# A graph layer on one core: x and edges also handed in transposed, first stage for G alone

## The reference

```python
Q = relu(x @ Wq + bq);  V = x @ Wv + bv                 # x: 6250 x 512, float32
Q = relu(layer_norm(Q));  H = sum(Q, axis=1, keepdims=True) ** 2
H = pi / (2 * 2 * (max(H) - min(H))) * H
c, s = Q * cos(H), Q * sin(H)
out = c @ (c.T @ V) + s @ (s.T @ V)
norm = c @ sum(c, axis=0)[:, None] + s @ sum(s, axis=0)[:, None] + 1e-10
# edges: src, dst (106250, sorted by dst), and one loop of each node
deg = segment_sum(ones, dst);  coef = rsqrt(deg)[src] * rsqrt(deg)[dst]
gcn = segment_sum((x @ Wg)[src] * coef, dst) + bg
y = relu(layer_norm(out / norm + gcn + V) * gamma + beta)
return layernorm(x + y)
```

## Time and profile before

| | us |
|---|---|
| median of 3 runs (lowest to highest) | 1565.83 (1563.94 to 1568.54) |
| span of the profiled execution, first to last instruction | 1564.0 |
| TensorE matmuls busy, x7911 | 1493.1 (95%) |
| VectorE busy | 1060.7 (68%) |
| GpSimd busy | 921.2 (59%) |
| ScalarE busy | 497.6 (32%) |

### The profile page before, as it was taken

The page is one execution under the profiler, slowest core; times in us unless marked ns, Lnnn a source line. Parts: engine busy times, 40 slices in busy tenths (PEclk is TensorE's granted clock), DMA queues, the critical chain, the costliest instruction groups (busy, mean ns, idle before and its releaser), DMA issues.

```text
span 1564.0 us, 24480 instructions
## 1 busy us (share of the span) xinstructions
PE 1493.1 (95%) x7911; PEld 942.9 (60%) x7911; DVE 1060.7 (68%) x2945; ACT 497.6 (32%) x1010; POOL 921.2 (59%) x1022
## 2 busy tenths in 40 slices
PE   5999999899999997999998999989999999999995
PEld 3777788666666663444443444437777777767763
DVE  6999577677777676444445544457878877878785
ACT  2322776533333222111111111113333333333332
POOL 0000000277777775777776777777777777777772
PEclk9999999999999997999999999999999999999997
DMA  6555544699999998889888999889999999999894
GB/s 237 183 183 183 175 157 150 235 311 311 331 309 331 299 325 246 286 286 302 284 285 260 292 296 307 294 248 314 298 290 311 304 294 294 312 288 309 279 315 130
DMA packets 172753, 423.84 MB, mean 271 GB/s; under 512 B 24142, under 2 KB 25802, under 8 KB 172616
## 3 DMA queue, kind: packets, MB, share of 16 engines
q0 software_dynamic: 71120, 236.74, 48.1%
q1 hardware_dynamic: 79980, 146.16, 27.3%
q10 hardware_dynamic: 21516, 39.29, 6.6%
HBM read 351.42 MB, written 70.67 MB: 270 GB/s over the span
## 4 chain that ended last, share of the span: by engine, by line
PE 83%; DMA 6%; DVE 6%; issue 2%; ACT 2%; POOL 1%; SPq 0%; POOLq 0%; DVEq 0%; ACTq 0%
PE bank L1320 18%; PE bank L1321 17%; PE bank L1322 17%; PE bank L1436 12%; PE bank L1438 11%; DMA gathered<-scaled_g,index_slots 3%; DVE stage L948 2%; PE bank L1567 1%; PE bank L1376 1%; DMA stage<-in_x 1%; PE bank L1363 1%; POOL gathered L550 1%; DMA combine<-values 1%; PE bank L1504 1%; PE bank L1507 1%
## 5 line engine op out<-in xcount | busy, mean ns | idle before, releaser
L550 POOL DMA_INDIRECT gathered<-scaled_g,index_slots x882 | 882.9, 1001 | 305.7 <-issue 187.7
L1066 DVE TENSOR_SCALAR one_hot<-iota_bf,dst_in_tile,gathered 128x128 bf16<-128x128 bf16 x882 | 268.8, 326 | 327.4 <-DMA gathered<-scaled_g,index_slots 300.5
L1320 PE MATMUL bank<-weights,operands 128*128 128x512 f32 x784 | 395.5, 504 | 6.6 <-DVE stage L966 6.1
L1436 PE MATMUL bank<-gathered,one_hot 128*128 128x512 f16 x882 | 344.1, 390 | 25.7 <-DVE one_hot L1066 25.6
L1438 PE MATMUL bank<-gathered,one_hot 128*128 128x512 f16 x882 | 339.0, 384 | 0.0
L1321 PE MATMUL bank<-weights,operands 128*128 128x512 f32 x784 | 311.3, 397 | 0.0
L1322 PE MATMUL bank<-weights,operands 128*128 128x512 f32 x784 | 310.7, 396 | 0.0
L535 POOL COPY dst_slots<-dst_cols 128x18 f32 x49 | 13.9, 284 | 301.8 <-issue 299.6
L1320 PEld LDWEIGHTS bank<-weights,operands 128*128 128x128 f32 x784 | 149.1, 190 | 69.4 <-DVE stage L966 7.0
L1436 PEld LDWEIGHTS bank<-gathered,one_hot 128*128 128x128 bf16 x882 | 85.9, 97 | 171.1 <-issue 74.9
L707 ACT ACTIVATE operands_f<-operands,cos_sin_v 128x512 f16<-128x512 f32 x98 | 69.5, 720 | 335.8 <-PE bank L1322 201.6
(11 more groups left out here) (231 smaller groups left out, 1916.3 us busy)
## 6 DMA issues: line engine op xcount, KB each, us to landing
operands<-values SPq DMA_DIRECT2D x98, 256.0 KB, 5.7
stage<-in_x SPq DMA_DIRECT2D x96, 256.0 KB, 3.8
turned_x<-operands SPq DMA_DIRECT2D x37, 512.0 KB, 3.1
operands<-turned_x SPq DMA_DIRECT2D x37, 512.0 KB, 6.4
gathered<-scaled_g,index_slots POOLq DMA_INDIRECT x882, 5.2
scaled_g<-pairs SPq DMA_DIRECT2D x49, 260.0 KB, 2.1
pairs<-scaled_g SPq DMA_DIRECT2D x49, 260.0 KB
values<-stage ACTq DMA_DIRECT2D x49, 256.0 KB, 4.8
```

Source lines behind the costliest of these rows:

```text
L550: pool.indirect_dma_start(out=plain(row_ring[k % RING]), out_offset=None, in_=table, in_offset=bass.IndirectOffsetOnAxis(ap=index_slots[:, ...
L1066: dve.tensor_scalar(one_hot[:, k % HOT, :], iota_bf[:, :], column(dst_in_tile, seq % 2 * PER_TILE + k), scale_of(row), ALU.is_equal, ALU.m ...
L1320: pe.matmul(out_ap, a_hi, b_hi, start=start and n == 0, stop=False, skip_group_check=True)
L1436: pe.matmul(gcn_banks[seq % 2][:, :], one_hot[:, k % HOT, :], hi, start=k == 0, stop=False, skip_group_check=True)
```

## The change

- The host hands in, beside x, x in transposed tiles (`x_turned`), src and dst with a column for each chunk of 128 edges (`src_by_chunk`, `dst_by_chunk`), and dst padded (`dst_flat`). The transposes of x and of the edges on TensorE, their copies out of PSUM, and the DRAM copy of the transposed x go.
- First stage: SP loads the transposed tile to where the rest will be, four tiles in turn, when the tile four before is multiplied. ScalarE rounds it (`g_round`), GpSimd subtracts the rounded part from it in place (`g_split`), before which GpSimd waits for src and copies it. VectorE waits for GpSimd's tile t before the compares of tile t.
- All 49 tiles of Q and V are in the run, one every 16/3 steps. SP loads the transposed x again (256 KB), ScalarE rounds it (`x_round`), VectorE subtracts (`x_split`). The square of V moves from VectorE to ScalarE.
- The own row is added to V from G in SBUF when V is made (`own_sum`) and stored (`own_values`); `own_load` and `add_own` go, and the combine load takes that sum.
- The sweeps are spread over the steps anew: 20/7 steps a tile for cosine and sine, 27/4 for the output.

The core of the diff:

```diff
-    FUSED = 12
-    QV_TILES = TILES - FUSED
     QV_RING = 3
     STEPS = TILES * PER_TILE
-    HEAD, DRAIN = 6 * QV_RING, 24
-    LAST_QV = 6 * (QV_TILES - 1 - QV_RING)
+    HEAD, DRAIN = 18, 24
+
+    def qv_at(t):
+        return 16 * (t - QV_RING) // 3
+
+    LAST_QV = qv_at(TILES - 1)
...
-    COS_END = COS_AT + 10 * (TILES - 1) // 3 + 3
+
+    def cos_at(t):
+        return COS_AT + 20 * t // 7
+
+    COS_END = cos_at(TILES - 1) + 3
     SIN_AT = COS_END + 6
-    SIN_END = SIN_AT + 3 * (TILES - 1) + 3
+
+    def sin_at(t):
+        return SIN_AT + 20 * t // 7
+
+    SIN_END = sin_at(TILES - 1) + 3
     OUT_AT = SIN_END + 6
-    assert B == 4 and TAIL and FULL == 48 and SCALED < QV_TILES and OUT_AT + 7 * FULL < STEPS
+
+    def out_at(n):
+        return OUT_AT + 27 * n // 4
+
+    assert B == 4 and TAIL and FULL == 48 and out_at(FULL) + 7 < STEPS and qv_at(0) >= -HEAD
...
             def g_load(t):
-                r, n = rows_of(t), x_slot(t)
-                if t in (WIDE + 2, WIDE + 3):
-                    sp.wait_ge(s["degrees_summed"], 1)
-                else:
-                    sp.wait_ge(s["g_x_turned"], freed(t, 2 if t < WIDE + 2 else 4))
-                sp.dma_start(stage[0:r, n, :], dram_rows(x, t, r)).then_inc(g_x_loaded[n], 16)
+                sp.wait_ge(s["g_summed"], freed(t, XT_RING))
+                sp.dma_start(operands_raw[:, 4 + t % XT_RING, :], x_turned[t, :, :]).then_inc(g_x_loaded[t % XT_RING], 16)
 
             def raw_load(raw, weight, arrived):
                 sp.dma_start(raw, weight.rearrange("(k p) n -> p k n", p=P)).then_inc(s[arrived], 16)
 
-            g_load(0)
-            g_load(1)
-            full_groups(src, src_nat, s["src_loaded"])
-            last_group(src, src_nat, s["src_loaded"])
+            sp.dma_start(dst_i, dst_by_chunk).then_inc(s["dst_loaded"], 16)
+            for t in range(XT_RING):
+                g_load(t)
             raw_load(raws[1], Wq, "q_raw_loaded")
             raw_load(raws[2], Wv, "v_raw_loaded")
+            sp.dma_start(src_i, src_by_chunk).then_inc(s["src_loaded"], 16)
...
+            def x_load(t):
+                if t < XT_RING:
+                    sp.wait_ge(s["g_summed"], done(TILES - XT_RING + t))
+                else:
+                    sp.wait_ge(s["q_summed"], freed(t, XT_RING))
+                sp.dma_start(operands_raw[:, 4 + qv_slot(t), :], x_turned[t, :, :]).then_inc(x_loaded[t % XT_RING], 16)
...
             for t in range(0, TILES):
-                if t <= WIDE:
-                    g_load(t + 2)
-                if t == WIDE:
-                    g_load(t + 3)
-                if t >= WIDE and t + 4 < TILES:
-                    g_load(t + 4)
-                if t < QV_TILES:
-                    xt_store(t)
+                if t + XT_RING < TILES:
...
-                if seq == 0:
-                    sp.wait_ge(s["v_squared"], done(FUSED - 1))
+                sp.wait_ge(own_stored[seq % QV_RING], 16 * (seq // QV_RING + 1))
                 sp.wait_ge(s["combined_stored"], seq * 16)
-                sp.dma_start(combine[:, :], dram_rows(values, seq, P)).then_inc(s["combine_loaded"], 16)
+                sp.dma_start(combine[:, :], dram_rows(own_values, seq, P)).then_inc(s["combine_loaded"], 16)
...
+            pool.wait_ge(s["src_loaded"], 16)
+            pool.tensor_copy(src_cols[:, :], src_i).then_inc(s["src_kept"], 1)
+            pool.sem_inc(s["g_x_split"], LEAD)
+
+            def g_split(t):
+                rest, raw = operands[:, 4 + t % XT_RING, :], operands_raw[:, 4 + t % XT_RING, :]
+                pool.wait_ge(s["g_x_hi"], done(t))
+                pool.tensor_tensor(rest, raw, plain(operands[:, t % XT_RING, :]), ALU.subtract)\
+                    .then_inc(s["g_x_split"], 1)
+
+            for t in range(TILES):
+                g_split(t)
 
...
-            def g_step(t, n, r):
-                turned = banks[1 + n][:, :].rearrange("p (b c) -> p b c", c=P)[:, :, 0:r]
-                x_hi = operands[:, t % 4, :].rearrange("p (b c) -> p b c", c=P)[:, :, 0:r]
-
-                act.wait_ge(s["g_x_turned"], done(t))
-                act.wait_ge(s["g_summed"], freed(t, 4))
-                if t - 4 < QV_TILES:
-                    act.wait_ge(xt_stored[t % 4], t // 4 * 16)
-                else:
-                    act.wait_ge(s["q_summed"], done(nth(t - 4)))
-                act.copy(x_hi, turned).then_inc(s["g_x_hi"], 1)
-
-            def g_keep(t, n, r):
+            def g_round(t):
+                act.wait_ge(g_x_loaded[t % XT_RING], t // XT_RING * 16 + 16)
+                act.copy(operands[:, t % XT_RING, :], operands_raw[:, 4 + t % XT_RING, :]).then_inc(s["g_x_hi"], 1)
+
+            def x_round(t):
+                act.wait_ge(x_loaded[t % XT_RING], t // XT_RING * 16 + 16)
+                act.copy(operands[:, qv_slot(t), :], operands_raw[:, 4 + qv_slot(t), :]).then_inc(s["x_hi"], 1)
...
+            def own_store(t):
+                act.wait_ge(s["own_summed"], done(t))
+                act.dma_start(dram_rows(own_values, t, P), own_room(t)).then_inc(own_stored[t % QV_RING], 16)
+
+            def v_square(t):
+                act.wait_ge(s["v_kept"], done(t))
+                if t > 0:
+                    act.wait_ge(s["v_squared"], done(t - 1))
+                act.activation(squares_out, v_room(t), ACT.Square, accum_out=column(row_v_square, t))\
+                    .then_inc(s["v_squared"], 1)
 
...
-                for t, at in in_flight(qv_at, QV_TILES, q):
+                for t, at in in_flight(qv_at, TILES, q):
+                    if at == 1 and t + 1 < TILES:
+                        x_round(t + 1)
+                    if at == late(t, 5):
+                        v_store(t)
+                        v_square(t)
                     if at == 6:
-                        v_store(t)
+                        own_store(t)
...
-            def g_split(t, n, r):
-                turned = banks[1 + n][:, :].rearrange("p (b c) -> p b c", c=P)[:, :, 0:r]
-                x_hi = operands[:, t % 4, :].rearrange("p (b c) -> p b c", c=P)[:, :, 0:r]
-                x_lo = operands[:, 4 + t % 4, :].rearrange("p (b c) -> p b c", c=P)[:, :, 0:r]
-                dve.wait_ge(s["g_x_hi"], done(t))
-                dve.tensor_tensor(x_lo, turned, plain(x_hi), ALU.subtract).then_inc(s["g_x_split"], 1)
+            def x_split(t):
+                rest, raw = operands[:, 4 + qv_slot(t), :], operands_raw[:, 4 + qv_slot(t), :]
+                dve.wait_ge(s["x_hi"], done(t))
+                dve.tensor_tensor(rest, raw, plain(operands[:, qv_slot(t), :]), ALU.subtract)\
+                    .then_inc(s["x_split"], 1)
...
+            def own_sum(t):
+                if t == 0:
+                    for n in range(PAIRS):
+                        dve.wait_ge(pair_stored[n], 16 * len(range(n, TILES, PAIRS)))
+                dve.wait_ge(own_stored[t % QV_RING], t // QV_RING * 16)
+                dve.wait_ge(s["v_kept"], done(t))
+                dve.scalar_tensor_tensor(own_room(t), q_tile(t), column(own_scale, t), v_room(t), ALU.mult, ALU.add)\
+                    .then_inc(s["own_summed"], 1)
...
-            g_split(0, 0, P)
-            g_split(1, 1, P)
             for t in range(0, TILES):
+                dve.wait_ge(s["g_x_split"], done(t))
                 if t < HIST_TILES:
-                    bins(3 * t)
-                keep_beside_g(t)
-                if t + 2 < TILES:
-                    g_split(t + 2, t % 2, rows_of(t + 2))
-                if t < HIST_TILES:
-                    bins(3 * t + 1)
-                    bins(3 * t + 2)
-                beside_g(t)
+                    for third in range(3):
+                        bins(3 * t + third)
                 between_tiles(t)
             for n in range(pairs_until(TILES - 2), pairs_until(TILES - 1)):
                 pair_split(n)
             for group in FACTOR_GROUPS:
                 if group[2] == TILES:
...
-            def add_own(seq):
-
-                dve.wait_ge(s["combine_loaded"], seq * 16 + 16)
-                dve.wait_ge(s["own_loaded"], seq * 16 + 16)
-                link = linked("own_linked", seq, 1)
-                hi, lo = halves(own_rows)
-                link(dve.scalar_tensor_tensor(combine[:, :], hi, column(own_scale, seq), combine[:, :],
-                                              ALU.mult, ALU.add))
-                dve.scalar_tensor_tensor(combine[:, :], lo, column(own_scale, seq), combine[:, :],
-                                         ALU.mult, ALU.add).then_inc(s["own_added"], 1)
-
...
-            def qv_beside_g(t):
-                if t == QV_TILES:
-                    pe.wait_ge(s["raw_split"], 1 + 2 * B)
-                else:
-                    pe.wait_ge(s["v_kept"], done(nth(t) - 1))
-                x_product(banks[5], t % 4, range(B), 2).then_inc(s["v_summed"], 1)
-                if t > QV_TILES:
-                    pe.wait_ge(s["q_biased"], done(nth(t) - 1))
```

(15 more changed lines are left out.)

366 lines of the change are left out of this document (123 added, 243 removed).

## The result

| | us |
|---|---|
| median after (4 runs, 1579.27 to 1582.29) | 1580.19 |
| median before, beside it (4 runs, 1563.94 to 1568.56) | 1567.18 |
| ratio, 95% interval | 1.0091, 1.0076 to 1.0106 |
| span of the profiled execution after | 1578.4 |

The change makes the kernel 0.9% slower. The forecast was 1590 with a range of 1560 to 1613; it had the right direction, and 1.5% where 0.9% was measured.

A forecast was written before the change was run, and what follows sets the result against it. TensorE was taken to bound the run, TensorE and VectorE together tiles 0 to 30, and ScalarE tiles 31 to 48 after the change. 0.4 + 5.5 − 40.2 + 58.0 = +23.7 us on 1564.0, plus 1.8, gave 1590 us, range 1560 to 1613.

The forecast's parts named there:

- the forecast's closing sentence: Whole kernel: Q and V moved out cost the run 67.6 us; the stage they leave, held by ScalarE, shrinks less.
- Start: Before the first products: GpSimd's first subtraction waits behind its copy of src, products at 21.6 instead of 21.25, +0.4 us.
- Tiles 0 to 30: First stage: VectorE's 105 us and 31 GpSimd subtractions paid one after the other, 143.4 against 137.95 us, +5.5.
- The step that decided: Tiles 0 to 30: GpSimd's subtraction and VectorE's two-operand compares exclude each other, 1.12 + 2 × 0.06 us a tile.
- Tiles 31 to 48: Rest of G until Q and V start: ScalarE sets the pace, 89.8 against 130.0 us, −40.2.
- G's own part: Tiles 31 to 48: 13.0, 53.7 and 11.2 us for tiles 31 to 34, 35 to 44, 45 to 48, plus 5.7 of store waits.
- The idle chain: Between G and the run: TensorE idles 6.2 us for keep, square, factors, last halves, then new rounding and split of x.
- The run: The 882 steps: twelve moved tiles of Q and V at 5.63 us add 67.6, less vanished waits, +58.0 us.
- the forecast's list of 3.8, 3.3 and 2.5: Run savings in us: wait at its head; own-row additions and last one-hot at the end; TensorE idling in the sine sweep.
- The subtraction beside the compares: Rival, tiles 0 to 30: TensorE's 119 us sets them, 23 us less, 1566 us, no change; chance 0.13.
- That the run takes the work for nothing: Rival, run: gathers, not TensorE, set the steps and the 67.6 us fall into waits, 1522 us; chance 0.09.
- the third: Rival: subtraction costs 2.2 us a tile, 1623 us, chance 0.07; or stores stall ScalarE as often as now, 1600.

The follow-up runs named there:

- e11: Kernel before with turned x loaded, TensorE's transposes of x gone and the subtraction on GpSimd; edges still turned on chip, Q and V not moved: 1559.84 us.
- e4: Changed kernel with every tile's square taken on ScalarE as soon as the tile is kept: 1568.03 us.
- e6: Changed kernel with three edits: subtraction on VectorE, squares as soon as a tile is kept, first x of the run prepared ahead: 1541.42 us.
- e1: Changed kernel with the first stage's subtraction of rounded x made by VectorE again instead of GpSimd: 1558.55 us.
- e8: Kernel before with turned x loaded and TensorE's transposes of x gone, subtraction on VectorE; edges still turned on chip, Q and V not moved: 1556.56 us.
- e2: Changed kernel with GpSimd making the same subtraction once more, into an unread room, in tiles 0 to 30: 1615.98 us.
- e3: Changed kernel with a GpSimd memset of 128x512 in an unread room ahead of each subtraction in tiles 0 to 30: 1579.44 us.
- e7: Changed kernel with 4 of the 24 products of each tile's Q and V left out: 1540.11 us.
- e5: Changed kernel with the first x of the run loaded, rounded and split while tile 48 of G is being made: 1572.47 us.
- the best one: Changed kernel with subtraction on VectorE, early squares, first x prepared ahead, and four VectorE chunk-limit instructions moved behind tile 31: 1539.38 us.

## Why the prediction came out right, and where it was off

**The direction and its reason.** The forecast said that the Q and V moved out cost the run, and that the stage they leave can't shrink by as much, since ScalarE holds it. From e11 to the changed kernel Q and V move, and with them comes the rest of the change (the edges' turning, the stored transposed x and the reloaded own rows go, the sweeps are spread anew), which no run takes apart: the run grows by 50.3 us, tiles 31 to 48 shrink by 31.0, with +3.6 at the start and −1.2 in tiles 0 to 30, 21.7 in all. e4 and e6 show that it was ScalarE's hold and the order at its end that kept the stage at 90.58 us: without them it is 69.16. So what the forecast said of the run and of that stage holds. It is not the whole reason, though the forecast's closing sentence names no other: from e1 to the changed kernel the subtraction's place alone costs 22.9 us of span, and e1, with Q and V moved, is 0.4% faster than before. The subtraction on GpSimd without the move (e11) and the move without it (e1) are each faster than before; together they are slower. With the subtraction on VectorE the move is nearly neutral, 1558.55 (e1) against 1556.56 (e8): the run grows by 50.3 us there too, but the stage falls by 42.2, since e8's is held at 130 (by its own waits, as far as these tell). The forecast had priced each part against the kernel before and never against the other part left out, so it did not see this.

**Start**, +0.4 forecast, −0.9 measured. The forecast's order is right (src's copy ahead of the subtraction), and e1, at 17.31, shows that this order costs 3.1 us; but src landed earlier than the 19.5 us reckoned, since its copy starts at 18.18, and the copy and the first subtraction took 0.93 and 1.24 us, near the 0.9 and 1.1 forecast.

**Tiles 0 to 30**, +5.5 forecast, +3.7 measured. The step that decided, that the subtraction and the compares exclude each other, was taken from two small copies and is confirmed by e1, e2 and e3. Its price of 1.12 + 0.12 us was a little high: VectorE loses 1.03 for each, or 0.97 by busy time (30.0/31). The duration taken for the subtraction was low, 1.26 us at shortest against 1.12; its mean of 1546 ns contains its own waiting. So the 141.61 us are 107.4 of other work on VectorE, 30.0 of drawn-out compares and 4.2 of idle time, where the forecast had 105 and 38.4. A tile took 141.61/31 = 4.57 us, within the 4.4 to 4.9 named.

**Tiles 31 to 48**, −40.2 forecast, −39.9 measured, and this is luck: two errors cancel. G's own part was put at 77.9 + 5.7 = 83.6 us, with the 5.7 for stored pairs, and took 77.98 (162.00 to 239.98), with 2.7 us of such waits on ScalarE; ScalarE's period of 3.24 us in tiles 31 to 34 was right (it keeps at 164.90 and 168.15). The idle chain was put at 6.2 and took 12.60: the term names keep, square, factors, halves and the new rounding and split, and prices none of them by itself. The trace has two things that it does not name: ScalarE comes to keep the last tile only at 242.74, 2.8 us after TensorE's last product, since it is still at halves of earlier pairs; and the last half waits 1.91 us for the store of an earlier pair, with the rounding of x behind it.

**The run**, +58.0 forecast, +51.5 measured, the largest error. TensorE's busy time grew by 64.3 us for the 288 matmuls, 0.223 each, where the forecast had 5.63/24 = 0.235; e7 gives 0.218. The 36 matmuls and 40/176 us of the earlier trace rows were right, but the price of the chunks' matmuls was taken from the sweep and the whole rest put on Q and V; that this is where the 0.012 us a product come from is inferred, no run has the chunks' price beside Q and V. And the time in which TensorE is not busy fell from 48.4 to 35.6 us, by 12.8, where the forecast's list of 3.8, 3.3 and 2.5 has 9.6. The difference lies in the Q and V part with its head, where it fell by 6.9 (14.6 to 7.6 us) and not by 3.8.

**The rivals.** The subtraction beside the compares would have been 1566: e1 and e2 refute it. That the run takes the work for nothing is refuted by e7, where 196 products less gave 42.7 us. Of the third, neither half came: a subtraction costs 1.03 us and not 2.2, and ScalarE's waits for stored pairs fell from 22.7 us to 4.6 between tile 31 and the run.

## What to carry to other kernels

- Before work goes from VectorE to an idle GpSimd, look at what VectorE does at the time and with how many operands in SBUF. GpSimd's busy share says nothing: at 50 of 141.6 us it cost more than it took over.
- A change of several parts is to be forecast in pairs, each part with and without the other. Here the turned x with either of the two other parts alone was 0.3 to 0.4% faster than before, and with both 0.9% slower.
- When work leaves a stage, ask which engine is next there, and pull forward its instructions that have no need to wait, in the stage and at its seam. By order alone, e4 and e5 gave 12.2 and 7.7 us singly, of the 40.8 between the changed kernel and the best one.

## What was not expected of the hardware

- A GpSimd copy that reads one operand of 128x512 (0.61 us at shortest, 0.92 on average beside the compares) costs VectorE's two-operand compares only 0.38 to 0.41 us, a subtraction that reads two (1.26 at shortest, 1.55 on average) costs 0.91 to 1.03, and a memset of the same shape, 0.53 us, none.
- The exclusion shows in no wait. The trace has it as a longer mean of the same instruction, 570 to 741 ns, and as a longest compare of 1.85 us where e1 has 0.76, and VectorE looks busier than it is.
